# Reordering the quantisation and the turned copies inside the steps of a fused adaLN attention and MX feed-forward kernel

## What is computed

```python
mod = (silu(c) @ wmod).reshape(8, 6, 1, 256)          # sa, ca, ga, sb, cb, gb
h = layernorm(x) * (1 + ca) + sa
q, k, v = h @ Wq.T + bq, h @ Wk.T + bk, h @ Wv.T + bv  # 16 heads of 16
raw = einsum('blhd,bmhd->bhlm', q, k)
scores = where(mask, raw, 0) / 4                       # mask: j = i, or i - 2**k
x = x + ga * (softmax(scores) @ v @ Wo.T + bo)
h = layernorm(x) * (1 + cb) + sb
xq, xs = mx_quantize(h)       # blocks of 32: xs = max|h| / 7.5, xq nearest of the FP6 values
wq, ws = mx_quantize(weight)
x = x + gb * ((xq * xs) @ (wq * ws).T + bias)
```

## Time and profile before

| | |
|---|---|
| median of three runs | 305.88 us (305.63 to 306.06) |
| the profiled execution's own time | 306.11 us |
| its span in the trace | 304.4 us |
| TensorE's mean granted clock | 0.948 of full speed |
| busy: DVE, PE, POOL, ACT | 268.7, 259.2, 216.5, 206.9 us |

### The profile page before, as it was taken

The page is one execution under the profiler, slowest core; times in us unless marked ns, Lnnn a source line. Parts: engine busy times, 40 slices in busy tenths (PEclk is TensorE's granted clock), DMA queues, the critical chain, the costliest instruction groups (busy, mean ns, idle before and its releaser), DMA issues.

```text
span 304.4 us, 4341 instructions
## 1 busy us (share of the span) xinstructions
PE 259.2 (85%) x1324; PEld 161.5 (53%) x1324; DVE 268.7 (88%) x348; ACT 206.9 (68%) x551; POOL 216.5 (71%) x154
## 2 busy tenths in 40 slices
PE   3898995998969868989998999899979758998394
PEld 1654453366536613664566457645755346875273
DVE  3879699969998999899999999999999989989821
ACT  1586775877797976987998799766747264637310
POOL 6101529984989989799989998999998999514200
PEclk9999996999999997999999999999979966999879
DMA  7633975794964389236962694369437942302024
GB/s 239 170 149 100 358 203 178 245 349 123 338 165 129 103 251 300 91 103 200 330 200 83 217 329 134 79 227 322 134 106 215 302 138 72 98 6 86 1 71 138
DMA packets 54387, 53.90 MB, mean 177 GB/s; under 512 B 4094, under 2 KB 52812, under 8 KB 54364
## 3 DMA queue, kind: packets, MB, share of 16 engines
q1 hardware_dynamic: 54364, 53.63, 56.6%
HBM read 44.89 MB, written 8.72 MB: 176 GB/s over the span
## 4 chain that ended last, share of the span: by engine, by line
DVE 47%; PE 22%; issue 11%; POOL 9%; ACT 7%; DMA 2%; SPq 0%; DVEq 0%; POOLq 0%; ACTq 0%
DVE prod L1402 18%; DVE pv_buf L1517 12%; POOL pv_buf L588 5%; PE ps L885 5%; DVE prod L1391 3%; PE ps L849 3%; PE ps L710 2%; PE ps L787 2%; ACT x_norm L988 2%; DVE ps L1410 2%; DMA pv_buf<-in_L_wmod 2%; DVE ps L1489 1%; DVE ps L1493 1%; DVE ps L1488 1%; PE ps L817 1%
## 5 line engine op out<-in xcount | busy, mean ns | idle before, releaser
L588 POOL TENSOR_TENSOR pv_buf<-pv_buf 128x1024 f32<-128x1024 f32 (+2 forms) x63 | 137.8, 2187 | 21.0 <-DVE pv_buf L1517 16.7
L1402 DVE TENSOR_TENSOR prod<-ps,kT 128x1024 f32<-128x1024 f32 (+4 forms) x70 | 75.4, 1112 | 0.0
L1517 DVE TENSOR_TENSOR pv_buf<-v_shift,ps 128x1024 f32<-128x1024 f32 x49 | 59.5, 1214 | 0.0
L805 PE MATMUL ps<-prod,sel_sum 128*32 128x512 f32 x256 | 31.9, 621 | 7.0 <-DVE prod L1402 7.0
L849 PE MATMUL ps<-wo_g,w_raw 128*128 128x256 f32 x128 | 33.4, 406 | 0.0
L710 PE MATMUL ps<-hT,wT 128*128 128x512 f32 x64 | 30.7, 622 | 0.9 <-ACT hT L1078 0.8
L737 PE MATMUL ps<-wT,h_cen 128*128 128x256 f32 x128 | 29.6, 379 | 0.0
L721 PE MATMUL ps<-hT,wT 128*128 128x512 f32 x64 | 29.4, 600 | 0.0
L849 PEld LDWEIGHTS ps<-wo_g,w_raw 128*128 128x128 f32 x128 | 24.1, 198 | 6.7 <-issue 3.9
L737 PEld LDWEIGHTS ps<-wT,h_cen 128*128 128x128 f32 x128 | 24.0, 190 | 6.5 <-issue 3.8
L885 PE MATMUL ps<-wf_g,w_raw 128*128 128x256 f32 x80 | 20.5, 400 | 0.0
(11 more groups left out here) (180 smaller groups left out, 552.9 us busy)
## 6 DMA issues: line engine op xcount, KB each, us to landing
v_shift<-v_rows SPq DMA_DIRECT2D x56, 512.0 KB, 5.4
x_in<-in_L_attn_x SPq DMA_DIRECT2D x8, 512.0 KB, 3.9
v_rows<-v_base SPq DMA_DIRECT2D x8, 512.0 KB, 4.3
x_res<-in_L_attn_x SPq DMA_DIRECT2D x8, 512.0 KB, 6.4
out_x<-outb SPq DMA_DIRECT2D x5, 512.0 KB, 5.2
rows_mod<-mod_rows SPq DMA_DIRECT2D x7, 256.0 KB, 3.2
x<-in_L_wmod SPq DMA_DIRECT2D x1, 1024.0 KB, 6.3
row_ga<-mod_rows SPq DMA_DIRECT2D x8, 128.0 KB, 4.4
```

The lines of the kernel that those rows point to most:

```text
L588: nc.gpsimd.tensor_tensor(dst, dst, ring(b, n)[:, t:NT, :], ALU.add).then_inc(s_add, 1)
L805: mm = nc.tensor.matmul(ps23[32 * g:32 * g + 32, 1, :], sel_sum[:, which, c, :], prod[:, n, c, :], start=(c == 0 and which == 0), stop=(c ...
L1402: nc.vector.tensor_tensor(prod[:, n, :, o:L], ps01[:, :, o:L], kT[:, b % 2, :, 0:L - o], ALU.mult).then_inc(s_prod, 1)
L1517: nc.vector.tensor_tensor(dst[:, t:NT, :].rearrange("p t (h e) -> p t h e", e=DH), v_n.rearrange("p t (h e) -> p t h e", e=DH), weights, A ...
```

## The change

- DVE: `block_maxima(b - 2)` goes from the middle of the step to its end. `quantise` goes from the end of step b-1 into step b, between `softmax_max` and `softmax_weights`, where `dequantise` stood. `dequantise` goes behind the fourth pv product. In the last part `quantise(4)` stands in the softmax and `dequantise(4)` behind the first pv product.
- ACT: `quantised` goes from the start of the step behind `evacuate_attention`. `evacuate_v(b + 1, 0)` moves into the middle of `evacuate_attention`, and `evacuate_xd` between the two `evacuate_k`.
- PE: attention's transposes go between the two halves of v. The transposes of xd go between the two halves of k.
- The reciprocal is kept in SBUF (`inv_kept`) and copied to PSUM (`q_inv`) ahead of the division. The scale is written to PSUM in `ps45` up to batch 3.

```diff
@@ buffers
-        amax, mx_inv = (by_t[:, i, (NS + 2) * HEADS:(NS + 2) * HEADS + NT * NB] for i in range(2))
-        dq_scale = ps67[:, 0, NS * HEADS:NS * HEADS + NT * NB]
+        amax, mx_inv, dq_scale = (by_t[:, i, (NS + 2) * HEADS:(NS + 2) * HEADS + NT * NB] for i in range(3))
+        q_inv = ps67[:, 0, NS * HEADS:NS * HEADS + NT * NB]
+        inv_kept = sb("inv_kept", [P, NT * NB])
@@ PE
             def attention_transposes(b):
                 pe.wait_ge(s_vm, b + 1)
-                if has(b - 2):
+                if b == LAST - 1:
                     pe.wait_ge(s_xdT, b - 1)
+                elif has(b - 2):
+                    pe.wait_ge(s_z, b - 1)
...
             def xd_transposes(b):
                 pe.wait_ge(s_xd, b + 1)
-                if b <= TAIL:
-                    pe.wait_ge(s_d, b + 4)
-                    pe.wait_ge(s_vm, b + 3 if b < TAIL else B)
+                if b < TAIL:
+                    pe.wait_ge(s_x1, b + 3)
+                elif b == TAIL:
+                    pe.wait_ge(s_d, B)
+                    pe.wait_ge(s_vm, B)
...
                 v_rows(b + 1, 1)
-                if post:
-                    xd_transposes(b - 3)
-                v_rows(b + 1, 0)
                 if has(b - 1):
                     attention_transposes(b - 1)
+                v_rows(b + 1, 0)
...
                 if ahead:
                     k_rows(b + 2, 1)
+                if post:
+                    xd_transposes(b - 3)
+                if ahead:
                     k_rows(b + 2, 0)
@@ ACT
             for b in range(LAST):
...
-                if has(b - 3):
-                    quantised(b - 3)
                 exps(b)
...
                 evacuate_v(b + 1, 1)
-                if has(b - 3):
-                    evacuate_xd(b - 3)
                 if b == 0:
                     norm_before(2)
-                evacuate_v(b + 1, 0)
-                if has(b - 1):
+                    evacuate_v(b + 1, 0)
+                else:
                     evacuate_attention(b - 1)
+                if has(b - 3):
+                    quantised(b - 3)
...
                     evacuate_k(b + 2, 1)
+                if has(b - 3):
+                    evacuate_xd(b - 3)
+                if ahead:
                     evacuate_k(b + 2, 0)
...
+            exps(LAST)
             quantised(LAST - 3)
-            exps(LAST)
@@ DVE
                 softmax_max(b)
                 if has(b - 3):
-                    scale_to_psum(b - 3)
-                    dequantise(b - 3)
+                    inverse_to_psum(b - 3)
+                    quantise(b - 3)
                 softmax_weights(b)
...
                 pv_product(b, 3)
+                if has(b - 3):
+                    dequantise(b - 3)
                 qk(2, 3)
-                if has(b - 2):
-                    block_maxima(b - 2)
...
                 pv_product(b, 9)
                 if has(b - 2):
-                    quantise(b - 2)
+                    block_maxima(b - 2)
 
             softmax_max(LAST)
-            scale_to_psum(LAST - 3)
+            inverse_to_psum(LAST - 3)
+            quantise(LAST - 3)
+            softmax_weights(LAST)
+            pv_product(LAST, 0)
             dequantise(LAST - 3)
-            softmax_weights(LAST)
-            for n in range(6):
+            for n in range(1, 6):
                 pv_product(LAST, n)
```

More of the change, by code:

```diff
@@ L249, in adaln_block @@
         s_z = sem("zq_ready")
-        s_scale = sem("scale_in_psum")
+        s_scale = sem("inverse_in_psum")
         s_q8 = sem("q8_ready")
@@ L863, in xd_transposes @@
                     for c in range(NC):
-                        mm = nc.tensor.transpose(ps67[:, c, P * t:P * t + P], xd[:, t, P * c:P * c + P], ident[:, :])
+                        mm = nc.tensor.matmul(ps67[:, c, P * t:P * t + P], xd[:, t, P * c:P * c + P], ident[:, :],
+                                              start=(t == 0), stop=(t == NT - 1), is_transpose=True,
+                                              skip_group_check=True)
                 mm.then_inc(s_xdTp, 1)
@@ L1136, in evacuate_attention @@
                                          bias=v_mean[:, b % 2, c:c + 1]).then_inc(s_att, 1)
+                if has(b + 2):
+                    evacuate_v(b + 2, 0)
+                for c in range(NC):
                     act.wait_ge(s_att, NC * b + c + 1)
@@ L1155, in seed_ffn @@
                 act.wait_ge(s_x1, b + 3)
+                act.wait_ge(s_xdT, b + 1)
                 for k2 in range(2):
@@ L1407, in block_maxima @@
                 n = upto_half(b, half_)
-                src, scale = (h2, mx_scale) if b < LAST else (h2_last, scale_last)
+                src = h2 if b < LAST else h2_last
+                scale = dq_scale if b < TAIL else mx_scale if b < LAST else scale_last
+                inv = inv_kept if b <= TAIL else mx_inv
                 dve.wait_ge(s_h2, n)
@@ L1412, in block_maxima @@
                 dve.wait_ge(s_post, NPOST * n - 2)
+                if 0 < b < TAIL:
+                    dve.wait_ge(s_xd, b)
                 nc.vector.tensor_scalar(scale[:, g], amax[:, g], TO_E4M3 / FP6_MAX, TO_E4M3 * MX_EPS,
@@ L1415, in block_maxima @@
                 dve.wait_ge(s_post, NPOST * n - 1)
-                nc.vector.reciprocal(mx_inv[:, g], scale[:, g]).then_inc(s_post, 1)
+                nc.vector.reciprocal(inv[:, g], scale[:, g]).then_inc(s_post, 1)
             def quantise(b, half_=None):
@@ L1424, in quantise, with inverse_to_psum @@
                 src, dst = (h2, xd) if b < LAST else (h2_last, zq_last)
+                inv = q_inv if b <= TAIL else mx_inv
                 nc.vector.tensor_tensor(dst[:, t, :].rearrange("p t (g k) -> p (t g) k", k=BLOCK),
                                         src[:, t, :].rearrange("p t (g k) -> p (t g) k", k=BLOCK),
-                                        over(mx_inv[:, g], BLOCK), ALU.mult).then_inc(s_z, 1)
-            def scale_to_psum(b):
-                nc.vector.tensor_copy(dq_scale, mx_scale[:, :]).then_inc(s_scale, 1)
+                                        over(inv[:, g], BLOCK), ALU.mult).then_inc(s_z, 1)
+            def inverse_to_psum(b):
+                nc.vector.tensor_copy(q_inv, inv_kept[:, :]).then_inc(s_scale, 1)
                 dve.wait_ge(s_scale, b + 1)
@@ L1436, in dequantise @@
                 src, dst = (q8, xd) if b < LAST else (q8_last, zq_last)
-                scale = scale_last if b == LAST else dq_scale if b <= TAIL else mx_scale
+                scale = scale_last if b == LAST else dq_scale if b < TAIL else mx_scale
                 nc.vector.tensor_tensor(dst[:, t, :].rearrange("p t (g k) -> p (t g) k", k=BLOCK),
```

## The result

The changed kernel takes **309.49 us** (median of four runs, 308.37 to 310.19) against 305.97 (305.63 to 306.37): ratio 1.0102, 95% interval 1.0074 to 1.0129. It is slower by about 1%. Applied to the 305.88 us known at the forecast, the ratio gives 309.0 us; the forecast was 307.8, with a range of 306.3 to 309.2. So the sign was right, the size too small by 1.2 us, and the median itself lies just above the range. Two executions that took far longer than the rest, one of 1448.02 us in experiment 5's second kernel and one of 392.35 us of the kernel before in experiment 7's session, are left out of the medians, ranges and ratios here.

A forecast was written before the change was run, and what follows sets the result against it. DVE was taken to bound the steps and PE's chain the part after them. Steps gain 3.91 us, turned xd of batch 4 loses 5.61, net +1.70 on 306.11: 307.8 us, range 306.3 to 309.2.

The forecast's parts named there:

- Step 2: With the maxima out of its middle, batch 3's softmax starts 1.78 us earlier, bound by DVE.
- Steps 3 to 5: DVE's wait of 0.43 us ahead of dequantisation goes in each step, 1.29 us in sum.
- rival 1: Steps don't shrink, since late turned xd holds up PE's scores: price 0.66 to 1.29 us, 308.5 to 309.1; chance 0.20.
- rival 4: Exponentials' gap isn't filled: ACT so late that DVE still waits after the division; no chance of its own.
- Turned xd of batch 4: After the last step, PE starts these transposes 9.08 us behind batch 7's softmax, 5.61 us later than before.
- Rival 3: Last part starts at PE's full clock, so 5.15 us of work take 2.58: 305.2 us; chance 0.07.
- Step 6: Dequantisation's wait shrinks by 0.22 us and q-k products end earlier, so batch 7's softmax gains 0.84 us.
- S + 30.39: Forecast start of batch 7's softmax, both by PE's scores and DVE alone; S is the start of step 6's softmax.
- S + 26.94 - 0.84: Forecast start of PE's last head sums in step 6, with the softmax following 4.29 us later.
- the stretch of before, moved along: PE's low-clock stretch around the last part's start, 5.15 us of work at 0.50, taken as unchanged but later.
- rival 2: A short slow stretch, 3.20 us of work at the lower clock: 306.8, or up to as much slower; chance 0.13.
- No difference, 0.1 us either way: Small operands moving between SBUF and PSUM cost nothing, within 0.1 us per batch, half a us in sum.

The follow-up runs named there:

- experiment 5: Changed kernel plus idle matmuls on PE in step 6 whose result nobody reads: seven, 309.21 us; in its second kernel three, 309.89 us.
- experiment 7: Tests of whether batch 4's scale and reciprocal lie in SBUF or PSUM, on several kernels; times under 7a, 7b and 7c.
- experiment 3: Kernel before with only the block maxima moved to the step's end, ahead of the division: 304.58 us, ratio 0.9939.
- experiment 1: Changed kernel's steps with the last part ordered as before, batch 4's reciprocal read from SBUF: 303.8 us, ratio 0.9924.
- experiment 2: Kernel before with only the last part's order changed, batch 4's reciprocal kept in SBUF: 311.49 us, ratio 1.0164.
- 7a: Changed kernel with three idle matmuls in step 6 and batch 4's scale copied to PSUM again: 308.86 us, ratio 1.0085.
- experiment 4: Changed kernel with attention's transposes and ACT's evacuation put back behind both halves of v: 309.79 us, ratio 1.0106.
- 7c: Batch 4's reciprocal and scale in PSUM again: first on experiment 1's kernel, 304.21 us; then on the kernel of 302.29 us, 302.69 us.
- experiment 6: Kernel before with four idle matmuls in the last part, three ahead of turned xd of batch 4 and one behind: 304.86 us, ratio 0.9951.
- 7b: Kernel before with one edit, batch 4's dequantise reading its scale from SBUF without the copy to PSUM: 306.38 us, ratio 1.0015.
- the kernel of 302.29 us: Changed kernel's steps with the old last part, plus idle matmuls: three in step 6, five in the last part; ratio 0.9863.

## Why the forecast was right, and where it was short

**Right, by its own steps.** Step 2: 1.74 for 1.78. Steps 3 to 5: 1.30 for 1.29, with no idle time ahead of the division, the dequantisation or softmaxes 4 to 6, so rivals 1 and 4 fell for these steps. The gain itself did not need the division's new place: the wait of 0.43 us was gone with the maxima's move alone (experiment 3). Turned xd of batch 4: 5.61 later behind its softmax, as computed. Everything behind it on PE followed, and the net sign with it. Experiments 1 and 2 show the last part's price. Rival 3 (PE at the full clock when turned xd starts) fell too: 0.50 until 260.

**The step that failed: "*Step 6* ... S + 30.39 ... So 0.84".** It took 31.94, 1.55 more. The term that failed is the start of PE's last head sums, S + 26.94 - 0.84 = S + 26.10: they began at S + 27.67, and from there the softmax followed 4.27 us later (4.29 forecast). So rival 1's outcome, DVE waiting for PE's scores, did come in this step, by another cause. The forecast worked the end out from DVE and from head sums that start earlier, at durations of full speed, and looked for what was late in PE's order only in `k` and the feed-forward. It did not ask what PE does while it waits. With turned xd late in the step, PE idled 4.3 us in three pieces, its clock went to 0.50 at 226, and head sums and feed-forward took 1.72 and 0.74 us longer. DVE's own work in step 6 is 30.34 to 30.35 us (experiments 7a and 4, no idle time ahead of softmax 7), so 30.39 was right for DVE. The clock stayed at 1.00 there in all five kernels that had idle matmuls in step 6; without them it fell near 226 to 227 in the changed kernel and in those of experiments 1 and 7c (the first one), and earlier in experiment 4. The kernel before had a low stretch in step 6 as well (its projection took 3.49 us at 225.39), which cost nothing there: step 6 took 31.23 us, and 31.33 and 31.44 in experiments 6 and 7b, which have the same steps and kept the full clock. I had its 0.94 in the earlier trace rows and did not follow it up.

**The clock's term, "the stretch of before, moved along".** It was 1.07 us longer. Here rival 2 named the right mechanism, a stretch of another length, and priced it mainly on the wrong side. Turned xd to the 58 transposes took 12.43 us in the profile before; in nine other kernels without idle matmuls in that part it took 12.74 to 13.99, among them 13.77 in experiment 7b, whose steps are those of before; PE's order in that part is the same in all. The five in which turned xd starts 3.5 to 3.9 us behind softmax 7 (before, experiments 1, 3, 7b and the first of 7c) have a mean of 13.18 us, the six in which it starts 9 us or more behind it 13.55. So about 0.4 us may be the change's and the rest of the 1.07 the low value of the one profile before; each is a single execution, so this split is argued and not shown. Of the start of a kernel the Trainium skill (TensorE: Matmul & The Clock Gate, What's actually happening) says that the number of slow matmuls varies from run to run. For whole executions of one kernel the runs here agree: 22 of the kernel before, in experiment 7's session, took 305.0 to 305.2 us where the mean granted clock was 0.961 and 305.9 to 307.4 where it was 0.948 or 0.949. The last +0.46 is of the same kind: a feed-forward half took 2.40 us at 296.88 where before it took 1.99.

**The start, -0.93**, is not the change's either. Softmax 1 began at 63.65, 62.92 and 62.75 us in experiments 2, 6 and 7b, which share the setup of before. It takes up 0.93 of the 1.53 us of the two terms above, by luck. Without these three rows the table leaves +3.24, between the 3.1 of the ratio and the 3.5 of the medians, and 1.54 above the forecast's 1.70. By these rows step 6's 1.55 is all of the miss.

**"No difference, 0.1 us either way" for operands moved between SBUF and PSUM.** For the changed kernel it was right by luck: GpSimd's operation ended at 250.19, 0.12 after the dequantisation of batch 4 began. Batch 5's, which reads SBUF in both kernels, took 1.79 us there and 1.22 before (264.30), while DVE had 4.73 us of idle time ahead of it. With DVE 1.2 to 1.6 us earlier, batch 4's took 2.41 or 2.79 (experiments 5 and 4).

What stays open is whether the times bear this out: the share of the 3.5 us between the medians that belongs to step 6. Without its delay softmax 7 came 1.6 us earlier behind softmax 6, but the median fell by only 0.6 us (7a against the changed kernel, with overlapping intervals).

## What to carry to other kernels

Judge a move by the part after the loop as well: the same order gained 3 us in the steps and lost over 5 where nothing else covered a dequantisation, and giving the last part its own order kept 2.3 us of the gain. Try the smallest move by itself too: the maxima alone gave most of it. When an edit makes an engine with a clock gate wait in pieces, price what it does next at both clocks, and take the price of a low-clock stretch from several executions, not from one. Ask of every VectorE instruction that ends up with all operands in SBUF what GpSimd is doing then.

## What was not expected of the hardware

A VectorE `tensor_tensor` of 128x1024 with all operands in SBUF took 1.22 us with no GpSimd instruction beside it (batch 5 in the kernel before, 264.30) and 1.79, 1.93, 2.41 and 2.79 behind one that had begun earlier. GpSimd's three adds took 5.74 us in the kernel before and 6.51 (experiment 2), 6.52, 6.59 and 7.57 where such instructions began ahead of one of them (7.57 in the kernel of 302.29 us, where two did). With one operand in PSUM neither paid anything (7a, 7c). And idle matmuls that nobody reads made the kernel before 0.5% faster: the clock fell while they ran, but PE was back at 2.4 GHz when its critical run began.
